# A gated cross-attention and expert kernel: filter in natural order, context turned round, first two Toeplitz tiles read from the input, x first, order replanned

## The reference, cut to what matters

```python
# long convolution "attention", k = v = context, q = layernorm(x)
kv  = einsum('bhil,bhjl->bijhl', k_, v_)          # 8 x 8 products per head
y   = causal convolution of kv with ssm_kernel[h]  # done by FFT in the reference
out = y + kv * D[h]
out = einsum('bijhl,bhil->bjhl', out, q_)
x   = x + tanh(g_xattn) * out
# mixture of experts, 8 experts, top 2, on z = layernorm(x)
gates   = top-2 softmax of z @ router_w + router_b, renormalised
combined = sum_e gates[e] * gelu(z @ expert_w[e] + expert_b[e])
x = x + tanh(g_ffn) * (combined @ out_w + out_b)
```

## Time and profile before

| | before |
|---|---|
| median of three runs | 115.87 us |
| profiled execution | 115.83 us, span 114.0 us |
| PE busy | 103.2 us (90%) |
| DVE busy | 90.2 us (79%) |
| POOL busy | 63.0 us (55%) |
| ACT busy | 57.2 us (50%) |
| chain that ended last | PE 61%, POOL 17%, DVE 13%, ACT 4% |

### The profile page before, as it was taken

One profiled execution on the slowest core, in us unless ns is written; L12 is line 12 of the kernel. 1 busy time (PEld: TensorE's weight loads), 2 busy tenths in 40 slices (PEclk: granted clock), 3 DMA queues, 4 the chain that ended last, 5 costly groups with the idle time before them and its releaser, 6 DMA issues.

```text
span 114.0 us, 1919 instructions
## 1 busy us (share of the span) xinstructions
PE 103.2 (90%) x574; PEld 86.3 (76%) x574; DVE 90.2 (79%) x293; ACT 57.2 (50%) x145; POOL 63.0 (55%) x83
## 2 busy tenths in 40 slices
PE   4956999989999999996679999999999999999960
PEld 4945888868999887754568888886788888888940
DVE  0283899999999998999889969777588876866940
ACT  4074377064258718641469997465645424353300
POOL 3015799999999999999999899600000000000000
PEclk9999999999999999999999999999999999999997
DMA  2867999159872410030030000000000101111031
GB/s 79 294 165 196 297 370 324 50 180 244 227 231 87 155 35 3 0 92 0 0 95 6 0 0 0 0 0 0 0 6 0 46 11 35 46 49 46 0 98 46
DMA packets 10956, 10.02 MB, mean 88 GB/s; under 512 B 1306, under 2 KB 10946, under 8 KB 10946
## 3 DMA queue, kind: packets, MB, share of 16 engines
q1 hardware_dynamic: 9570, 8.85, 26.6%
q10 hardware_dynamic: 1376, 1.05, 2.9%
HBM read 8.82 MB, written 1.07 MB: 87 GB/s over the span
## 4 chain that ended last, share of the span: by engine, by line
PE 61%; POOL 17%; DVE 13%; ACT 4%; issue 3%; POOLq 0%; DVEq 0%
PE ring L835 11%; PE ring L837 11%; PE ring L836 11%; POOL kv_t L374 10%; PE ring L756 6%; DVE zq_t L397 4%; PE ring L757 3%; PE ring L706 3%; DVE ow_lo_t L1040 2%; POOL w_lo_t L389 2%; ACT q_t L560 2%; PE red L779 2%; POOL rstd L403 2%; PE zbank L877 2%; PE red L712 2%
## 5 line engine op out<-in xcount | busy, mean ns | idle before, releaser
L1116 DVE SCALAR_TENSOR_TENSOR mix_t<-ring,ctxT_t,mix_t 128x256 f32<-128x256 f32 x55 | 26.6, 484 | 7.8 <-ACT ring L603 6.1
L603 ACT ACTIVATE ring<-ring 128x512 f32<-128x512 f32 (+1 forms) x33 | 18.7, 568 | 20.7 <-PE ring L837 20.7
L374 POOL TENSOR_TENSOR kv_t<-ctxT_t 128x320 f32<-128x320 f32 x27 | 23.7, 908 | 8.2 <-ACT ctxT_t L515 6.5
L835 PE MATMUL ring<-w_hi_t,zT_hi_t 128*128 128x512 f32 (+1 forms) x66 | 26.1, 396 | 0.0
L837 PE MATMUL ring<-w_hi_t,zT_lo_t 128*128 128x512 f32 (+1 forms) x66 | 25.4, 385 | 0.0
L836 PE MATMUL ring<-w_lo_t,zT_hi_t 128*128 128x512 f32 (+1 forms) x66 | 25.4, 384 | 0.0
L756 PE MATMUL ring<-kv_t,toep_t 128*128 128x288 f32 x64 | 20.9, 409 | 0.2 <-DVE zq_t L1021 0.2
L757 PEld LDWEIGHTS ring<-kv_t,toep_t 128*128 128x128 f32 x64 | 12.2, 190 | 3.3
L837 PEld LDWEIGHTS ring<-w_hi_t,zT_lo_t 128*128 128x128 f32 x66 | 12.4, 188 | 2.5
L835 PEld LDWEIGHTS ring<-w_hi_t,zT_hi_t 128*128 128x128 f32 x66 | 12.5, 189 | 2.3
L836 PEld LDWEIGHTS ring<-w_lo_t,zT_hi_t 128*128 128x128 f32 x66 | 12.5, 189 | 2.1
(11 more groups left out here) (124 smaller groups left out, 170.8 us busy)
## 6 DMA issues: line engine op xcount, KB each, us to landing
ctx_t<-in_L_ffn_expert_w SPq DMA_DIRECT2D x8, 256.0 KB, 4.3
toep_t<-kpad_dram SPq DMA_DIRECT2D x3, 512.0 KB, 6.6
x_t<-in_x SPq DMA_DIRECT2D x8, 128.0 KB
out<-x_t SPq DMA_DIRECT2D x8, 128.0 KB
wlast_t<-in_L_ffn_expert_w SPq DMA_DIRECT2D x1, 768.0 KB, 7.1
ctx_t<-in_ctx ACTq DMA_DIRECT2D x2, 256.0 KB, 3.0
zq_t<-in_x ACTq DMA_DIRECT2D x2, 256.0 KB, 3.7
ctx_t<-in_ctx SPq DMA_DIRECT2D x2, 256.0 KB, 4.2
```

The costliest lines, as they stand in the source:

```text
L374: eng.tensor_tensor(dst, head.unsqueeze(1).to_broadcast([P, HB + 1, HD * CB]), windows(ctxT_t, g, h, HB + 1), ALU.mult).then_inc(done, 1)
L603: act.activation(y, y, ACT.Gelu_apprx_tanh).then_inc(gelu_ready, 1)
L835: pe.matmul(y, hi, whi, start=(c == 0), stop=False)
L1116: dve.scalar_tensor_tensor(out=acc, in0=ring[n % RING][:, L * e:L * (e + 1)], scalar=gate, in1=acc, op0=ALU.mult, op1=ALU.add).then_inc(mi ...
```

## The change

The taps are loaded in their natural order straight into the padded rows, and POOL adds D to tap 0. The Toeplitz tiles are no longer backwards in their row index as against the outputs; instead the context is: ACT copies each quarter of the context with its positions reversed within each 128 (`turn`, four instructions of 128x512) before PE transposes it. Queries and residual become plain. Heads start at 1 (`item`), and the tiles of heads 1 and 2 are read straight from the input with an overlapping pattern; what this reads of the neighbouring head is set to zero by POOL (`affine_select`), and D is put on the diagonal by another `affine_select` on POOL and an addition on DVE (`add_direct`). The other five transfers of tiles follow through the scratch as before. x is first on ACT's queue, context halves 0 and 1 are on SP's queue. Contexts 2 and 3 are transposed behind convolution 1. DVE forms three product items, not five, and POOL 29, not 27. Group 1 has three folds, not four: two by DVE, one by POOL. DVE forms the low parts of experts 0 and 3, not of 5. The order on all engines is rewritten.

```diff
-TOEP = ((0, 1), (1, 3), (4, 4), (8, 4), (12, 4))
-BY_VECTOR = (0, 5, 15, 22, 27)
-
-RELATIVE_BY_DVE, LOW_BY_DVE = (), (5,)
-FOLDED_BY_DVE = ((2,), (2, 3))
-FOLDED_BY_POOL = ((), (0, 1))
-WARM_UP = (12, 1, 6, 1, 5, 5)
+FIRST, DIRECT = 1, 2
+TOEP = ((3, 2), (5, 3), (8, 4), (12, 4), (0, 1))
+BY_VECTOR = (1, 14, 25)
+
+RELATIVE_BY_DVE, LOW_BY_DVE = (), (0, 3)
+FOLDED_BY_DVE = ((1,), (0, 2))
+FOLDED_BY_POOL = ((), (3,))
+FOLDS = ((4, 0), (5, 1), (6, 2), (7, 3), (2, 0), (3, 1), (1, 0))
+WARM_UP = (14, 1, 12, 1, 1, 5)
...
+        def item(n):
+
+            return n // H, (n + FIRST) % H
...
-            sp.dma_start(taps[:, :], ssm_kernel).then_inc(taps_in, 16)
-            sp.dma_start(dcol[:, :], ssm_d.rearrange("(h a) -> h a", a=1)).then_inc(taps_in, 16)
-
-            sp.wait_ge(taps_reversed, 1)
+            sp.dma_start(kpad[:, P - 1:P - 1 + L], ssm_kernel).then_inc(taps_in, 16)
+            for i in range(2):
+                load(sp, cv, ctx_in, context_in, i)
+
+            src = bass.AP(ssm_kernel.tensor, FIRST * L - (P - 1), [[1, P], [L, DIRECT], [1, L]])
+            sp.dma_start(toep[:, FIRST:FIRST + DIRECT, :], src).then_inc(direct_in, 16)
+            sp.wait_ge(taps_ready, 1)
             sp.wait_ge(constants_ready, 1)
             sp.dma_start(scratch, kpad[:, :]).then_inc(scratch_written, 16)
             for i in range(2, LOADS):
                 load(sp, cv, ctx_in, context_in, i)
+            for i in range(2, LOADS):
+                load(sp, xn, x, x_in, i)
             sp.wait_ge(scratch_written, 16)
             for i, (h, n) in enumerate(TOEP):
-                src = bass.AP(scratch.tensor, h * (P + L), [[1, P], [P + L, n], [1, L]])
+                src = bass.AP(scratch.tensor, h * (P + L - 1), [[1, P], [P + L - 1, n], [1, L]])
                 sp.dma_start(toep[:, h:h + n, :], src).then_inc(toeplitz_in[i], 16)
-                if i >= len(TOEP) - 3 and i < len(TOEP) - 1:
-                    load(sp, xn, x, x_in, i - len(TOEP) + 5)
             last_rows(sp, 0, EARLY)
             sp.dma_start(rw, router_w.rearrange("(c p) n -> p c n", c=C)).then_inc(router_in, 16)
             sp.dma_start(rwlast[:, :], everywhere(router_w, (L - 1) * E, E)).then_inc(router_in, 16)
...
+            src, dst = FOLDS[i]
             terms = zq[:, g].rearrange("p i n a -> p i (n a)")
-            eng.tensor_tensor(terms[:, i], terms[:, i], terms[:, HB + i], ALU.add).then_inc(done, 1)
+            eng.tensor_tensor(terms[:, dst], terms[:, dst], terms[:, src], ALU.add).then_inc(done, 1)
...
+                pool.wait_ge(direct_in, 16)
+                within = toep[:, FIRST:FIRST + DIRECT, 0:P]
+                pool.affine_select(out=within, in_=within, compare_op=ALU.is_ge, fill=0.0, base=1 - P,
+                                   pattern=[[0, DIRECT], [1, P]], channel_multiplier=1).then_inc(direct_masked, 1)
                 pool.wait_ge(first_queries_ready, BG)
...
-            products(pool, 1, pool_products_ready)
+            pool.wait_ge(taps_in, 32)
+            pool.tensor_tensor(kpad[:, P - 1:P], kpad[:, P - 1:P], dcol[:, :], ALU.add).then_inc(taps_ready, 1)
+            pool.wait_ge(direct_d_in, 16)
+            pool.affine_select(out=added_d, in_=direct_d.unsqueeze(2).to_broadcast([P, DIRECT, P]), compare_op=ALU.is_equal,
+                               fill=0.0, base=1 - P, pattern=[[0, DIRECT], [1, P]],
+                               channel_multiplier=1).then_inc(added_d_ready, 1)
             first_inverse_std()
-            for n in range(2, 5):
-                products(pool, n, pool_products_ready)
-            for n in range(6, 15):
+            products(pool, 0, pool_products_ready)
+            for n in range(2, 14):
                 products(pool, n, pool_products_ready)
             scales(1)
-            for n in range(16, 22):
+            for n in range(15, 20):
                 products(pool, n, pool_products_ready)
             ones()
+            products(pool, 20, pool_products_ready)
+            relative(pool, 0, weights_relative)
+            for n in range(21, 25):
+                products(pool, n, pool_products_ready)
             router_relative_rows()
-            products(pool, 23, pool_products_ready)
-            relative(pool, 0, weights_relative)
+            products(pool, 26, pool_products_ready)
             relative(pool, 1, weights_relative)
-            weights_low(pool, 0, weights_low_ready)
+            relative(pool, 2, weights_relative)
+            products(pool, 27, pool_products_ready)
+            products(pool, 28, pool_products_ready)
+            scales(2)
+            for n in range(29, 32):
+                products(pool, n, pool_products_ready)
             weights_low(pool, 1, weights_low_ready)
-            for n in range(24, 27):
-                products(pool, n, pool_products_ready)
-            products(pool, 28, pool_products_ready)
-            products(pool, 29, pool_products_ready)
-            scales(2)
-            products(pool, 30, pool_products_ready)
-            products(pool, 31, pool_products_ready)
-            relative(pool, 2, weights_relative)
-            relative(pool, 3, weights_relative)
             weights_low(pool, 2, weights_low_ready)
-            fold(pool, 1, 0, pool_folded)
-            fold(pool, 1, 1, pool_folded)
-            weights_low(pool, 3, weights_low_ready)
+            for n in range(0, 3):
+                add_bias(n)
+            fold(pool, 1, 3, pool_folded)
+            add_bias(3)
+            for n in range(3, 7):
+                relative(pool, n, weights_relative)
+            for n in range(4, 7):
+                weights_low(pool, n, weights_low_ready)
+            relative(pool, 7, weights_relative)
+            scales(3)
+            weights_low(pool, 7, weights_low_ready)
             for n in range(4, 8):
...
-            for i in range(2):
-                load(act, cv, ctx_in, context_in, i)
-            for i in range(2):
-                load(act, xn, x, x_in, i)
+            load(act, xn, x, x_in, 0)
+            act.dma_start(dcol[:, :], ssm_d.rearrange("(h a) -> h a", a=1)).then_inc(taps_in, 16)
+            load(act, xn, x, x_in, 1)
+            act.dma_start(direct_d, everywhere(ssm_d, FIRST, DIRECT)).then_inc(direct_d_in, 16)
...
+            def turn(i):
+
+                act.wait_ge(context_in[i], 16)
+                start = CB * HD * P + B * L + BL * i * L
+                act.activation(backwards(zq_t, G * CB * HD * P, start),
+                               cv[:, BL * i:BL * (i + 1), :].rearrange("p b (c n) -> p b c n", c=C),
+                               ACT.Copy).then_inc(context_turned, 1)
...
-            for c in range(C):
-                evacuate(ctxT, red, context_transposed, 0, c, context_evacuated)
+            turn(0)
+            turn(1)
+            evacuate(ctxT, red, context_transposed, 0, 0, context_evacuated)
             act.wait_ge(gains_in, 32)
             act.activation(tgains[:, :], gains[:, :], ACT.Tanh).then_inc(tanh_ready, 1)
+            evacuate(ctxT, red, context_transposed, 0, 1, context_evacuated)
+            turn(2)
+            turn(3)
             half_gains()
+            evacuate(qT, (zbank, obank), queries_transposed, 0, 0, act_queries_evacuated)
             for c in range(C):
                 evacuate(ctxT, red, context_transposed, 1, c, context_evacuated)
-            evacuate(qT, (zbank, obank), queries_transposed, 0, 0, act_queries_evacuated)
...
+            statistics(B + 3)
+            split_weights(2)
             for n in range(0, 4):
...
+            scale_bias()
+            for n in range(0, 4):
...
+            split_weights(3)
+            statistics(B + 4)
             activate(3)
-            statistics(B + 4)
             split_weights(4)
+            split_weights(5)
             statistics(B + 5)
+            projection_high()
+            split_weights(6)
+            activate(4)
             statistics(B + 6)
-            activate(4)
-            split_weights(5)
+            activate(5)
             statistics(B + 7)
-            activate(5)
-            split_weights(6)
             activate(6)
+            activate(7)
             split_weights(7)
...
+                pe.wait_ge(context_turned, i + 1)
...
             warm_up(WARM_UP[0], ring[RING - 1])
-            for i in range(LOADS):
+            for i in range(2):
                 context(i)
                 warm_up(WARM_UP[i + 1], ring[RING - 1])
             queries(0)
             queries(1)
-            for n in range(0, 16):
+            convolve(0)
+            convolve(1)
+            context(2)
+            context(3)
+            for n in range(2, 16):
                 convolve(n)
             queries(2)
-            convolve(16)
-            convolve(17)
             queries(3)
-            convolve(18)
-            convolve(19)
-            for n in range(0, 3):
-                sum_channels(n)
+            for n in range(16, 20):
```

(62 more changed lines are left out.)

125 lines of the change are left out of this document (62 added, 63 removed).

## The result

The changed kernel takes **118.52 us** (median of 4 runs, 117.73 to 119.87) against 115.90 for the kernel before (4 runs): a ratio of 1.019 [1.012, 1.026]. I had said 114.0. The profiled execution took 118.56 us with a span of 116.7. Medians here are of all runs, ratios leave out the slow ones (over 1.5% above the fastest run of the same kernel), and the profiled executions of e1 and e8 are slow ones.

A forecast was written before the change was run, and what follows sets the result against it. PE bounds the kernel: time can be won only ahead of 12.49, in 2.73 us of idleness from 53.16 to 61.61, or by fewer or shorter matmuls. -1.6 + 1.0 - 0.2 - 2.0 + 1.0 = -1.8; 115.83 - 1.8 = 114.0 us, range 112.4 to 116.0.

The forecast's parts named there:

- F: Behind block 5: same matmuls on PE, mixture transposes move into cover; nothing, with 0.3 us either way.
- Rival (1): POOL falls behind ahead of block 0 through slower products, 3.4 us late, change slower at 117.4 us; chance 0.12.
- C: Rest of the filter up to block 0: waits of 0.7 us against 0.9, a gain of 0.2; block 0 at 44.7.
- A: Opening: x lands earlier, no product before POOL's root, first convolution at 10.9 against 12.49, gain 1.6 us (bounds 0.9, 2.2).
- my cover of 0.9 us: Opening, context leg: turns, transposes, copies and tanh done at 8.9, 0.9 us ahead of the queries at 9.8.
- the signs that I had named for being wrong: DVE or POOL at the folds after 48.5, PE waiting before block 0 for a low part, first convolution behind 12.
- B: Contexts 2 and 3: eight transposes, before at no cost, now stand behind convolution 1; costs 1.0 us.
- D: Gap before group 1's sums: folds in turn DVE, POOL, DVE, PE idle 1.3 us for 3.2, gain 1.9 to 2.0.
- E: Group 1's sums: one fold less, five slots not four, 8 matmuls at 0.123 us more, costs 1.0 us.

The follow-up runs named there:

- e1: The changed kernel with the bias row of expert 6 issued on SP ahead of expert 7's weights: 115.98 us, ratio 0.995.
- e8: The kernel before with x halves 0 and 1 ahead of context halves 0 and 1 on ACT's queue: 118.16 us, ratio 1.014.
- e2: The changed kernel with 30 idle transposes, not 12, between context 1 and the queries to keep PE busy: 117.74 us, ratio 1.013.
- e3: The changed kernel with contexts 2 and 3 transposed ahead of convolution 0, not behind convolution 1: 118.41 us, ratio 1.018.
- e4: The changed kernel with x half 1 issued ahead of the D column on ACT's queue: 117.63 us, ratio 1.012.
- e6: The kernel before with the rest of the output weights on DVE moved behind accumulate 4: 114.85 us, ratio 0.989.
- e7: The kernel before with e6's move, and POOL's second fold of group 1 dropped (ten matmuls per sum, not eight): 113.53 us, ratio 0.976.
- e11: The kernel before with POOL's inverse root ahead of its product 1: 116.41 us, ratio 1.004.
- e12: The kernel before with the edits of e7 and e11 together: 113.76 us, ratio 0.981.
- e5: The changed kernel with the queue moves of e1 and e4 together: 115.39 us, ratio 0.994.
- e10: The changed kernel with e9's edits, and contexts 2 and 3 transposed ahead of convolution 0: 115.02 us, ratio 0.993.
- e9: The changed kernel with e5's two queue moves, and POOL's fold of group 1 ahead of its biases 0 to 2: 115.43 us, ratio 0.996.

## Why the prediction was wrong, step by step

**F, behind block 5: costed at nothing, +2.1.** This is the failed step. I said that low parts 4 and 5 come from POOL at about 60 for a use at 63.8, and walked through POOL's and DVE's work, but not through SP's queue. Low part 3 had moved from POOL, where it stood at 54.43, to DVE behind the residuals, 58.82; with it moved the release of its buffer, the last weights that wait for it, and the bias row of expert 6 queued behind these. POOL then stood 3.28 us at that row with three low parts and the scales behind it. The prediction even had DVE's low part 3 done only at 57.9, and didn't ask who waits for it. e1 leaves the weights and DVE's low part where they are, moves the bias row alone, and takes 2.5 us off. Rival (1) had the change slower, with POOL late, by 3.4 us of slower products ahead of block 0. The products kept their pace; POOL's longer row did reach block 0 (see C), but the large loss came some fifteen us further on, through a wait and not through work. Without F the time would have been about 116, e1's, and still above my 114.0: the opening was wrong as well.

**A, the opening: -1.6 said, +0.5 measured, and another +1.5 through the clock.** The mis-sized term is x half 1: 7.15 for 5.8, and 6.67 to 7.15 in the four profiled executions with this order of ACT's queue (the changed kernel, e1, e2, e3). With the D column behind it (e4) it was 5.30; SP's loads moved in that run too. In the changed kernel's execution it is 1.35 of the 2.1 us by which convolution 0 came later than I had it; the root and the queries each came 0.2 later still behind what they wait for, and from the end of the queries (11.46) to convolution 0, where I had 1.1, it took 1.57, the last part of it waiting for POOL's first product. On top of that, convolutions 0 and 1 took 3.0 us at a clock of 0.50 where they take 1.46 at 1.00. I took the clock as 1.00 everywhere and did not ask what PE does while it waits for late queries. With half 1 at 5.30 (e4) the tanh on ACT became the end of the opening: my cover of 0.9 us wasn't there. Two of the signs that I had named for being wrong came true: the first convolution started behind 12, and both engines came to the folds behind 48.5 (DVE at 49.03, POOL at 51.09).

**B, contexts 2 and 3: +1.0 said.** From 16.04 to convolution 2 at 16.92: 0.9. Right, but it doesn't reach block 0 (e3).

**C, the filter: -0.2 said, -1.3 measured.** From convolution 2 to block 0 it takes 30.21 us after and 31.52 before, with the same matmuls in the program. The row of the filter in the earlier trace rows shows only 0.48 us of idle time before, since the modelled ends of matmuls cover short holes; the starts show them. The next pair begins 0.64 us behind 23.24 and 0.59 behind 24.44, where 0.25 is usual, and there are smaller holes at 42.47 and 42.89, 1.2 us in all:

```profile
23.88 0.72 PE L756 MATMUL ring<-kv_t,toep_t 128*128 128x288 f32 x2 [0.23 <-DVE zq_t L1021]
```

So A, B and C are not three terms to be summed. What block 0 follows, in all executions but one, is POOL's row of products behind the queries. From the start of that row to block 0 it takes 33.45 us before and 33.44, 33.48 and 33.45 in e6, e7 and e8, though the starts lie between 12.02 and 14.02; with one product more, 34.32 and 34.35 (e11, e12); with the changed kernel's work on POOL 35.24, 35.33, 35.32, 35.32 and 35.36 (e2, e3, e4, e5 and e10, all at a clock of 1.00 from 8.90 to 47). The changed kernel itself has 35.58, and in it POOL waits 0.26 for slow PE; e1 has 36.58, and in it such a wait of 1.28. Only e9, with 36.08, falls out of line, and I can't say why. By these rows the +1.66 at block 0 is POOL's start, 0.47 earlier (11.55 for 12.02), its work, 1.87 longer (three products and a relative pair more, two low parts fewer), and 0.26 for the clock. Against the prediction, which had 44.7, it is 1.75 for POOL's start (11.55 for 9.8), 0.4 for its work, 0.26 for the clock. It also says why e3 and e11 start the filter earlier in vain: they don't take work from POOL.

**D, the gap before sum 4: -2.0 said.** From block 0 to block 5 the change takes 14.77 us for 15.90, -1.13, and my D and E give -1.0. The size was right; the mechanism only in part, so some of it is luck. The idle time is 1.38 where I had 1.3, but the order is DVE, DVE, POOL where I had POOL in the middle, for POOL's three biases took 3.12 us instead of 2.2, beside DVE's folds. I also missed that the same two edits are worth 2.3 us without the rest (e7). Two differences can be the reason, and no run separates them. POOL has no biases in front of its fold in e7; e9, which moves them behind, brings PE's wait from 1.38 to 0.62 and not to nothing. And e7 keeps block 3 ahead of sum 4, where the change puts sum 4 first: a block lasts 1.39 us, as much as the wait. In e6 the rest of the output weights, moved out of the folds' way, shrinks from 2.85 to 1.40: that reading of the earlier trace rows held.

**E, the fifth slot: +1.0 said.** Ten matmuls in 1.36 us for a batch against eight in 1.13: 0.23 each time, four times, 0.9. Right.

Of the 2.7 us by which the span grew, then, 2.1 are F and 1.7 are the later block 0 (POOL's longer work, and 0.26 of it the clock), less the 1.1 that D and E win. How far the clock accounts for the 0.8 us between the medians of the changed kernel and e2 is open: the intervals overlap, and the profiled executions give it 0.3.

## What to carry to other kernels

When a step moves from one engine to another, follow what it releases as well as what it computes: here a buffer, the transfer that waits for the buffer, and every transfer queued behind that one. SP works through its list in order, so a small transfer that is wanted soon doesn't belong behind one that waits for something late. And before an opening is shortened, find out which engine's work sets the end of the stretch behind it; the cheapest test is to shift the start alone. Here an earlier first convolution won nothing, while the start of POOL's row came through one for one.

## What the runs showed of the hardware

- TensorE's clock: with PE busy 0.18 of the 2.10 us from 8.90 and 1.17 of the 2.00 us from 11.00, the granted clock fell to 0.50 in 13 to 16. With the first stretch filled (e2) it stayed at 1.00, and so it did with the first as empty as before (0.29) and only the second filled (e3), or with the second no fuller than before (1.17) and only the first filled (e4). So idle time of that length alone did not lower it in e3 (1.99 us there), and which of several things it takes is open: one of the changed kernel's own four runs kept a mean of 1.00.
- x half 1, 256 KB, landed between 6.67 and 7.15 when it was issued at 1.84 behind the D column (16 rows of 4 bytes) on the same queue, and at 5.30 when it was issued about 0.5 us earlier ahead of it (e4). SP's later loads also moved in e4, so the column alone isn't shown to be the reason.
- A fold of 128x1024 takes 1.23 us on DVE, and 2.40 on POOL where it starts first (e9). Beside one another each waits for the other's instruction: DVE's two folds end 2.2 us later than their own 2.5 us of work in e9, and POOL's one takes 3.34 in the changed kernel, where it starts second. This is what the Trainium skill says (SBUF — State Buffer, "two separate sides": the shared port pair is an exclusive lock, and whoever starts first has it for the whole instruction), and the trace agrees: POOL's fold has 2.40 us when it is first and 3.34 when it is second.
